# Attention with a gated FFN on one core: the four writes of squared q and k move from SP's queue to ScalarE's

## What is computed

```python
xn = _layernorm(x, axis=-1)
q = (xn @ Wq.T) ...; k = (xn @ Wk.T) ...; v = (xn @ Wv.T) ...
q = _rmsnorm(q, q_norm_w)
k = _rmsnorm(k, k_norm_w)
scores = jnp.einsum('bkgqd,bksd->bkgqs', qg, k) / math.sqrt(HD)
bias = jnp.where(rel > 0, NEG_INF, slopes[:, :, None, None] * rel)
attn = jax.nn.softmax(scores + bias[None], axis=-1)
out = jnp.einsum('bkgqs,bksd->bkgqd', attn, v)
s = out... @ Wo.T
g = _silu(_L0_ffn_ref(xn, ...))
x = x + s * g
```

## Time and profile before

| | us |
|---|---|
| median of 3 runs | 762.62 |
| lowest, highest | 760.61, 764.43 |
| the profiled execution | 757.6 |
| its span, first to last instruction | 755.8 |

### The profile page before, as it was taken

One profiled execution on the slowest core, in us unless ns is written; L12 is line 12 of the kernel. 1 busy time (PEld: TensorE's weight loads), 2 busy tenths in 40 slices (PEclk: granted clock), 3 DMA queues, 4 the chain that ended last, 5 costly groups with the idle time before them and its releaser, 6 DMA issues.

```text
span 755.8 us, 14611 instructions
## 1 busy us (share of the span) xinstructions
PE 718.8 (95%) x3736; PEld 608.6 (81%) x3736; DVE 602.9 (80%) x1468; ACT 561.8 (74%) x1440; POOL 364.3 (48%) x343
## 2 busy tenths in 40 slices
PE   7897999999999999999999999999999999999785
PEld 7786888878888788888888788887888788887665
DVE  7857798778978898678987789697987789788764
ACT  4566787696787788686877878776876967778662
POOL 4224354454544653554534743644544544446256
PEclk9999999999999999999999999999999999999999
DMA  8015969578686868787695777768685786867642
GB/s 298 1 29 143 299 154 255 164 221 241 168 273 152 239 185 245 198 225 228 163 283 144 220 214 222 228 167 268 162 250 167 221 236 176 265 153 196 195 134 83
DMA packets 215877, 148.68 MB, mean 197 GB/s; under 512 B 49072, under 2 KB 206640, under 8 KB 215728
## 3 DMA queue, kind: packets, MB, share of 16 engines
q1 hardware_dynamic: 215856, 148.43, 69.5%
HBM read 86.17 MB, written 62.19 MB: 196 GB/s over the span
## 4 chain that ended last, share of the span: by engine, by line
PE 56%; issue 13%; DVE 12%; POOL 8%; ACT 4%; SPq 3%; DMA 3%; POOLq 0%; DVEq 0%; ACTq 0%
PE qkv_ps L1266 6%; PE qkv_ps L1267 6%; PE qkv_ps L1268 6%; PE out_ps L1266 5%; PE out_ps L1268 5%; PE out_ps L1267 5%; PE score_ps L1266 4%; PE score_ps L1268 3%; PE score_ps L1267 3%; PE mix_ps L1266 3%; PE mix_ps L1268 3%; PE mix_ps L1267 3%; POOL w_lo L524 2%; PE turn_ps L1266 2%; SPq L449 2%
## 5 line engine op out<-in xcount | busy, mean ns | idle before, releaser
L551 POOL TENSOR_TENSOR pt_lo<-x_sb,pt_hi 128x512 fp32r<-128x512 f32 x137 | 174.3, 1298 | 240.6 <-ACT pt_hi L732 240.5
L669 ACT ACTIVATE probs<-probs,neg_max 128x128 f32<-128x128 f32 (+3 forms) x256 | 141.8, 556 | 62.0 <-DVE neg_max L949 61.6
L949 DVE CUSTOM_DVE_ANT_0 probs<-score_ps,cst,slope 128x128 f32<-128x128 f32 (+3 forms) x256 | 129.5, 546 | 34.0 <-PE score_ps L1268 25.6
L677 ACT ACTIVATE probs<-probs,recip 128x128 f32<-128x128 f32 (+3 forms) x252 | 126.3, 549 | 8.5 <-DVE recip L956 8.5
L1266 PE MATMUL qkv_ps<-w_hi,xt_hi 128*128 128x256 f32 (+1 forms) x392 | 126.0, 321 | 2.7 <-DVE xt_lo L892 1.4
L1267 PE MATMUL qkv_ps<-w_lo,xt_hi 128*128 128x256 f32 (+1 forms) x392 | 125.7, 321 | 0.0
L1268 PE MATMUL qkv_ps<-w_hi,xt_lo 128*128 128x256 f32 (+1 forms) x392 | 125.2, 319 | 0.0
L541 POOL TENSOR_TENSOR inv_rms<-sums,minus_half 128x5 f32<-128x5 f32 x64 | 78.8, 1231 | 78.6 <-DVE sums L1007 78.4
L1266 PE MATMUL out_ps<-wo_hi,o_hi 128*128 128x512 f32 x252 | 101.9, 404 | 3.3 <-DVE o_lo L993 3.3
L970 DVE STREAM_TRANSPOSE squared<-probs 128x256 f32<-128x256 f32 (+3 forms) x124 | 101.8, 823 | 2.0 <-ACT probs L677 1.1
L1267 PE MATMUL out_ps<-wo_lo,o_hi 128*128 128x512 f32 x252 | 100.2, 398 | 0.0
(11 more groups left out here) (172 smaller groups left out, 1637.5 us busy)
## 6 DMA issues: line engine op xcount, KB each, us to landing
turning_qk<-qk_squared SPq DMA_DIRECT2D x244, 80.0 KB, 1.9
qk_moved<-turning_qk SPq DMA_DIRECT2D x61, 320.0 KB, 3.4
turning<-squared SPq DMA_DIRECT2D x120, 128.0 KB, 2.4
x_sb<-turning SPq DMA_DIRECT2D x30, 512.0 KB, 5.1
w_raw<-wqkv SPq DMA_DIRECT2D x32, 384.0 KB, 5.5
turning<-squared SPq DMA_DIRECT2D x120, 96.0 KB, 2.0
x_sb<-turning SPq DMA_DIRECT2D x30, 384.0 KB, 4.2
turning<-squared SPq DMA_DIRECT2D x128, 64.0 KB, 1.8
```

The lines of the kernel that those rows point to most:

```text
L551: nc.gpsimd.tensor_tensor(by_quad(pt_lo, j), moved_block(t, j), by_quad(pt_hi, j).bitcast(F32), ALU.subtract).then_inc(pt_lo_by_pool, 1)
L669: nc.scalar.activation(probs[:, h, 0:n], probs[:, h, 0:n], ACT.Exp, bias=neg_max[:, h:h + 1], scale=-1.0, accum_out=total[:, h:h + 1]).the ...
L677: nc.scalar.activation(to[:, h, 0:n], probs[:, h, 0:n], ACT.Copy, scale=recip[:, h:h + 1]).then_inc(probs_ready, 1)
L949: nc.vector.tensor_tensor_reduce(probs[:, h, 0:n], score_bank(t, h), cst[:, C_DIST + SEQ - n:C_DIST + SEQ], slope[:, h:h + 1], HUGE, ALU.a ...
```

## The change

ScalarE gets a function `write_qk(g, u)`, with the wait and the four writes that stood at the head of `move`. It is called in ScalarE's slot behind the norms of heads 2 and 3 and ahead of the split of wo, `mixed_hi` and `moved_hi`; once more, for unit 3, ahead of the first slot. The SP queue goes straight to the probabilities. Semaphores and their values, shapes and the two reads stay.

```diff
@@ def move(g, t, u)
                 n = (i + 1) * P // 2
-                if u is not None:
-                    sp.wait_ge(qk_squared_ready, ONE(g, u - BY_TURN, 1))
-                    for q in range(QUADS):
-                        sp.dma_start(turning_qk[u % 2, q, :, :].rearrange("(k r) n -> r k n", k=QUADS),
-                                     qk_squared[q * QUAD:(q + 1) * QUAD, :, :]).then_inc(qk_written, 16)
                 for pair in range(2):
@@ ScalarE
+            def write_qk(g, u):
+
+                act.wait_ge(qk_squared_ready, ONE(g, u - BY_TURN, 1))
+                for q in range(QUADS):
+                    act.dma_start(turning_qk[u % 2, q, :, :].rearrange("(k r) n -> r k n", k=QUADS),
+                                  qk_squared[q * QUAD:(q + 1) * QUAD, :, :]).then_inc(qk_written, 16)
@@ ScalarE, def slot(g, t, left)
                 if here(t, left):
                     normalize_probs(g, t, range(2, HPG))
+                if here(t + 2, left):
+                    write_qk(g, t + 2)
                 if wo_due:
@@ ScalarE, ahead of the first slot
             moved_hi(0, 0)
+            write_qk(0, BY_TURN)
             slot(0, 2, GROUPS)
```

## The result

The changed kernel takes 756.1 us (755.52 to 757.56, five runs) against 762.8 (760.61 to 764.43, five runs): a ratio of 0.9918, 95% interval 0.9902 to 0.9935. So it is faster by 0.5 to 0.8%, where 783.6 us and a range from 764 to 800 had been forecast.

A forecast was written before the change was run, and what follows sets the result against it. TensorE bounds the kernel, working 85.16 of a group's 86.75 us. Losses of 0.9 + 1.6 + 0.5 = 3.0 us a group, seven times, make 21 us on the 762.62 us median: 783.6 us, range 764 to 800.

The forecast's parts named there:

- The price of one issue: Each write issued by ScalarE costs 0.45 us as on SP, 1.8 us for a block's four.
- I let none of it lie beside the norms: On ScalarE, all 1.8 us of a block's four issues delay its later work; none runs beside the norms.
- first rival: Issues run beside ScalarE's last two norms, hiding up to 1.0 us; 1.5 us a group lost, 773.1 us; chance 0.22.
- first place: Block with one key block and the next: pt_hi 1.35 us late, TensorE stands 0.9 us more a group.
- second place: Split of wo: the issues precede wo_hi, k_lo comes late, and TensorE loses 1.6 us a group.
- The forecast's sign: TensorE's waits for k_lo and w_lo were to rise from some 6 us to over 20.
- third place: Block splitting the next group's weights: ScalarE's square of k is late, w_lo follows, TensorE loses 0.5 us a group.
- I book this side at nothing: SP's shorter queue gains nothing; the read of q and k comes half a microsecond sooner at best.
- third rival: Issues are cheap and SP's shorter queue wins through earlier probability writes, about 5 us: 757.6 us; chance 0.05.
- The last sentence of the prediction: The forecast is wrong in size if the margins in the five other blocks are eaten as well.
- second rival: Issues cost ScalarE next to nothing, 0.4 us for four; only 1.4 us lost in all, 764.0 us; chance 0.12.

The follow-up runs named there:

- behind_norms: The changed kernel with one more wait ahead of ScalarE's four issues, until the last norm has ended; 807.44 us, ratio 1.059.
- no_writes: The kernel before without the four writes of q and k in the pipeline, so q and k are stale; 750.69 us, ratio 0.9864.
- half_each: The changed kernel with SP issuing two of the four writes at its old place and ScalarE the other two; 752.01 us, ratio 0.9876.
- extra_small: The kernel before with four added small writes (32 bytes a piece) by ScalarE at the changed kernel's place; 767.7 us, ratio 1.0078.
- small_before_read: The changed kernel with four added small SP writes between the probability writes and the read of q and k; 799.23 us, ratio 1.0486.
- half_again: half_each timed once more, beside the other splits on the same chip; 752.1 us, ratio 0.9863 against the kernel before.
- one_by_scalar: SP issues three of the four writes and ScalarE one, at the same places as in half_each; 763.4 us, ratio 1.0015.

## Why the prediction was wrong, step by step

- **The price of one issue** was right: 0.45 us forecast, 0.46 the median of 244 in the trace, 1.8 for four.
- **"I let none of it lie beside the norms"** is the step that failed first. The issues began within 0.05 us after the square in 50 of 61 blocks, and 58.7 of 108.5 us lay beside ScalarE's instructions. behind_norms makes the assumption true by force, and the kernel is 50 us slower than the changed one. The first rival named this and still took too little of it: it let the issues begin beside the last norms only, and nothing be hidden in the first place, where k_hi and both norms turned out to be overtaken. The evidence I used against it, 0.1 us between one start and the last end, was of two arithmetic instructions. It says nothing of an issue. What the Trainium skill, PSUM — Partial Sum Buffer, section Engine vs sequencer instructions, says of sequencer-only instructions as a class of their own agrees with the trace, though it doesn't name DMA issues among them. I gave the rival built on it 0.22.
- **The first and second place** did not come to pass. The forecast's sign was that TensorE's waits for k_lo and w_lo would go from some 6 us to over 20; they are 1.7 + 2.9 = 4.6. ScalarE's delay was smaller and its start earlier: in the block of the second place wo_hi begins at 329.68, behind 0.64 us of idle. Counted from the first scores of its group that is 0.3 us later than in rows 8 and not 1.8. ScalarE no longer waits 0.46 us for q and k in that block. GpSimd's wait for wo_hi is now 35.3 us in eight places and was 33.4: 1.9 more in all, and not 1.8 a time. The third place, booked at 0.5 us, shows 2.9 us of waits for w_lo in place of 2.2, 0.1 a time.
- **"I book this side at nothing"**, of SP's shorter queue, is the second failed step. The read of q and k did come "half a microsecond sooner" (0.6 in the mean), as forecast. But the relief is not worth nothing. no_writes takes 10 us less than before, with the writes' traffic gone as well; half_each takes 9 to 10 less with all traffic in place. I had argued that TensorE hardly waits for keys. What I missed is that ScalarE waits inside its fixed order for q and k, and everything behind it in that order, the norms, o_hi, pt_hi and the next squares, can move with it. In no_writes this wait is 16.4 us shorter. How the shorter wait becomes time of the whole kernel is argued and not traced step by step. The third rival had the direction and the size (757.6 forecast, 756.1 measured), but by luck, for the wrong reason: it held that it needs a nearly free issue and that the probabilities would do it. Its chance was 0.05.
- **The size of an unhidden delay** was too small as well. With nothing hidden the forecast had 3.0 us in a group and 21 in all; behind_norms has groups of 94.1 us, 7.2 longer than before, and takes 45.5 us more. TensorE waits there for VectorE's maximum in 13 places, about two in each group, a wait that the three places of the sum don't have. The last sentence of the prediction named this risk.
- **The rule of the second rival.** The Trainium skill, DMA: Bandwidth & Descriptors, section Issuing engines are not separate DMA queues, calls the issue time that several engines save usually small beside the transfer. In half_each the read went out 0.45 us sooner than before, and the kernel took 1.2 to 1.4% less: the small amount stood in front of the read that ScalarE waits for.

The two errors had the same sign. The loss was put at 21 us where the runs leave room for some 6 (changed kernel less no_writes, or extra_small less before), and the gain at nothing where they show 9 to 10. That is some 25 of the 27.5 us between 783.6 and 756.1. Both figures hold some traffic, so the split is an estimate.

## What to carry to other kernels

On ScalarE a DMA issue was not held up by the arithmetic ahead of it, only by the waits ahead of it: it started when its own semaphore and those in front were there. So charge only what outlasts the arithmetic, and check it by where the data become ready. Before booking a queue's relief at nothing, ask which engine with a fixed order waits for what the queue brings, and not whether TensorE does. And try to split a set of issues over two queues at the moment that their data are ready: two and two gave 1.2 and 1.4%, one on SP and three on ScalarE 1.2%, all four on ScalarE 0.5 to 0.8%.

## What the runs showed of the hardware

- ScalarE's issues overtook queued arithmetic instructions: k_hi and two norms in the block shown, up to four in others. They took 0.31 to 0.91 us each in the first trace (up to 1.42 in the second), 0.46 in the median of both; SP's same four took 0.32 to 1.02 before, 0.43 in the median.
- They did not overtake a wait. In small_before_read, where q_hi waited 2.17 us for its DMA, the issue behind it began 0.14 us after q_hi, 1.67 us after the square.
- Issues from both engines started in the same 0.01 us (306.57 in half_again), and neither was slower for it than alone: 0.80 us for two on SP, 0.36 and 0.46 on ScalarE.
- A second stream of 80 KB writes at the same moment raised the landing of the first from 1.9 to 2.9 us.
- Four added writes in each block, of 4 KB each (128 pieces of 32 bytes), cost 6 us even at the end of SP's moves, and raised the last landing of q and k from 4.1 to 4.6 us after the square.
- After pauses of TensorE of 1.39 us the granted clock fell to half for 3.41 us in two of six groups of one_by_scalar, and these groups were about 2 us longer.
